# Attention outputs kept transposed: no turns on PE, softmax sums inverted once per batch through DRAM, and the last expert rows of one tile weighted on PE

## What is computed

```python
x = x + 0.5 * ffn(layernorm(x))
x = x + attn(layernorm(x))
x = x + 0.5 * ffn(layernorm(x))

# attn: 32 heads of 16 for q, ONE head of 16 for k and v, ALiBi, causal
q = xn @ Wqkv[:, :512]; k = xn @ Wqkv[:, 512:528]; v = xn @ Wqkv[:, 528:]
scores = q k^T / 4 + slope_h * (pos_k - pos_q), causal
attn = softmax(scores) @ v            # [256, 32 heads * 16]
return attn @ Wo

# ffn: softmax router over 16 experts in 4 groups, 2 groups kept, 2 experts of them
y = sum over the 2 chosen e: gate_e * ((silu(x w1_e + b1) * (x w2_e + b2)) @ w3_e + b3)
return y + shared_expert(x)           # shared: 512 -> 256 -> 512
```

## Time and profile before

| | |
|---|---|
| median of 3 runs | 467.0 us (466.22 to 468.55) |
| the profiled execution, its time | 467.78 us |
| its span in the profile | 466.0 us |
| PE busy | 409.6 us, 88% |
| DVE busy | 261.9 us, 56% |
| ACT / POOL busy | 180.3 / 162.7 us |
| chain that ended last | PE 57%, DVE 15%, DMA 9%, SP's issues 9% |
| mean granted clock of PE | 0.97 of full speed |

### The profile page before, as it was taken

How to read it: one execution, slowest core, us unless ns; L and a number is a source line. 1 busy time by engine, 2 the same in 40 slices (tenths; PEclk the granted TensorE clock), 3 DMA queues, 4 the chain that set the end, 5 groups by cost and what they waited for, 6 DMA issues and landing times.

```text
span 466.0 us, 8466 instructions
## 1 busy us (share of the span) xinstructions
PE 409.6 (88%) x2848; PEld 289.0 (62%) x2849; DVE 261.9 (56%) x729; ACT 180.3 (39%) x300; POOL 162.7 (35%) x230
## 2 busy tenths in 40 slices
PE   0799879999959979879999899798999879999982
PEld 1687567888636757546665465343687558888650
DVE  5489513333258955868885785633239932333347
ACT  1321235665102221146663364483522316665300
POOL 2611316665302852333332242252000054666300
PEclk9999998999979999979999999999999989999987
DMA  7999973534296479212211200020120042444277
GB/s 213 312 372 313 322 234 129 171 108 158 99 364 191 129 181 194 75 39 73 74 56 26 69 6 6 0 74 24 46 91 1 1 134 79 171 132 147 95 269 305
DMA packets 48620, 63.88 MB, mean 137 GB/s; under 512 B 7750, under 2 KB 28070, under 8 KB 48548
## 3 DMA queue, kind: packets, MB, share of 16 engines
q1 hardware_dynamic: 40220, 41.51, 28.2%
q0 software_dynamic: 6368, 19.19, 12.8%
q10 hardware_dynamic: 2000, 2.76, 2.0%
HBM read 46.06 MB, written 19.79 MB: 141 GB/s over the span
## 4 chain that ended last, share of the span: by engine, by line
PE 57%; DVE 15%; DMA 9%; SPq 9%; issue 5%; POOL 2%; ACT 1%; ACTq 0%; POOLq 0%; DVEq 0%
PE ps L1453 14%; PE ps L1460 7%; PE ps L1607 6%; SPq L320 5%; PE ps L1579 5%; PE ps L1438 3%; DMA w<-in_L_ffn_ew_dram 3%; PE ps L1317 3%; PE ps L1522 3%; PE ps L1551 3%; DMA q_dram<-arena 2%; DVE arena L1159 2%; PE ps L1553 2%; PE ps L1565 2%; PE ps L1589 2%
## 5 line engine op out<-in xcount | busy, mean ns | idle before, releaser
L1159 DVE TENSOR_REDUCE arena<-ps 128x3 f32<-128x384 f32 x128 | 67.2, 550 | 17.5 <-PE ps L1553 16.7
L1453 PE MATMUL ps<-arena,wj 128*128 128x128 f32 x608 | 75.5, 278 | 0.0
L1453 PEld LDWEIGHTS ps<-arena,wj 128*128 128x128 f32 x608 | 72.6, 195 | 1.0 <-issue 1.0
L762 ACT ACTIVATE arena<-ps 128x768 f32<-128x768 f32 x64 | 51.8, 811 | 50.7 <-PE ps L1567 49.8
L592 POOL TENSOR_SCALAR_AFFINE_SELECT arena<-arena 128x512 f32<-128x512 f32 x64 | 40.8, 637 | 83.3 <-ACT arena L762 82.9
L1056 DVE SCALAR_TENSOR_TENSOR arena<-ps,arena 128x128 f32<-128x128 f32 x38 | 13.3, 351 | 87.6 <-ACT arena L678 87.6
L1317 PE MATMUL ps<-arena,turns 128*128 128x256 f32 x256 | 57.6, 381 | 0.0
L1317 PEld LDWEIGHTS ps<-arena,turns 128*128 128x128 f32 x256 | 48.2, 190 | 8.1 <-issue 2.1
L524 POOL DMA_INDIRECT y_dram<-arena x38 | 38.4, 1011 | 40.1 <-DVE arena L1063 31.6
L519 POOL DMA_INDIRECT arena<-xn_dram,arena x34 | 33.2, 977 | 51.4 <-DVE arena L996 25.2
L1460 PE MATMUL ps<-w,arena 128*128 x76 | 40.1, 611 | 4.0 <-DVE arena L1056 4.0
(11 more groups left out here) (190 smaller groups left out, 609.7 us busy)
## 6 DMA issues: line engine op xcount, KB each, us to landing
arena<-y_dram SPq DMA_DIRECT2D x16, 512.0 KB, 7.4
arena<-q_dram SPq DMA_DIRECT2D x36, 128.0 KB, 2.6
xn_dram<-arena SPq DMA_DIRECT2D x16, 256.0 KB, 5.8
w<-in_L_ffn_ew_dram SPq DMA_DIRECT2D x4, 1024.0 KB, 10.9
q_dram<-arena SPq DMA_DIRECT2D x16, 192.0 KB, 2.4
x<-_attn_hidden_states_dram SPq DMA_DIRECT2D x4, 512.0 KB, 6.0
...
```

The source lines that it names most:

```text
L762: act.activation(pr[:, n % 2, pair, :], ps[:, bank:bank + 2, :].rearrange("p a b -> p (a b)")[:, 0:768], ACT.Exp).then_inc(sem("exp"), 1)
L1159: dve.tensor_reduce(m3[:, h:h + 1, :], ps[:, bank, 0:3 * P].rearrange("p (n k) -> p n k", n=3), AX_X, ALU.max).then_inc(sem("s_max"), 1)
L1453: ins = pe.matmul(o, wj[:, par, c, n * INTER:(n + 1) * INTER], xgT[:, par, c, :], start=(c == 0), stop=(c == KC - 1))
```

## The change

**Attention without turns.** The output of four heads stays transposed. `vv` now holds v and ones interleaved (1, v0, 1, v1, ...): an even n takes 32 columns from the second on and gets values on the even partitions and the row's sum on the odd ones, an odd n the other way round. ACT copies an even n into `aT[b % 2][:, c, :]` (c = n // 2 % 4) and an odd n into `odd`. SP then moves, SBUF to SBUF: the sums of the even (`sums_of_even`), the sums of the odd and the odd values into their places (`odd_in`, two DMAs). The rows of Wo are loaded in the matching order, in two DMAs. `turn_back`, `attn_turn`, `turned`, `normalise(n)` are gone.

**Sums per batch.** For batches 0 to 2, DVE inverts the packed sums of a batch with one reciprocal of 128x256 (`invert`, in the next batch's q = 2); SP writes them to `r_dram` and reads them back with eight broadcasting DMAs (`inverses`); DVE multiplies the batch's 128x1024 outputs with one instruction (`normalise(b)`, at q = 4). For batch 3 the sums are copied to all rows at once and each pair of groups is inverted and multiplied alone (`normalise_last(c)`).

**Output product.** `out_part(b, t, c)` is a quarter of `out_product`: batches 0 and 1 have theirs in q = 5 (two between s1 and s2), and after the groups 5, 6 and 7; batch 2 after the groups 5 and 6 of the last batch; batch 3 one in the last group and the rest at the end. `max_turn(0, 1)` with its DVE work moves from ahead of the loop into group 0. `residual`, `row_stats`, `ln_stats` and `ln_rows` are spread over other groups.

**FFN.** `y_rows` of tiles 4 to 6 wait for six instead of eight `shared_up`; `shared_h(7)` stands before `pairs_x(1)` in FFN 0. In FFN 1, ACT makes two diagonal matrices of tile 6's gates (`weighing`), and PE adds the tile's expert rows with them to the shared output in PSUM (`rows_in(6)`), so that `pairs_x(6)` is gone and `shared_x(6)` comes after `pairs_x(5)`.

```diff
@@ ffn_sp
-            nc.sync.wait_ge(sem("s_gu"), NT * f + NT)
-            y_rows(range(4, NT))
+            nc.sync.wait_ge(sem("s_gu"), NT * f + NT - 2)
+            y_rows(range(4, NT - 1))
+            nc.sync.wait_ge(sem("s_gu"), NT * f + NT)
+            y_rows((NT - 1,))
@@ att_sp
+            def sums_of_even(p):
+                b, c = p // KC, p % KC
+                last = b + 1 == BATCH
+                sp.wait_ge(sem("oT"), 2 * p + 1)
+                if last and c >= 2:
+                    sp.wait_ge(sem("normed"), b + c - 1)
+                into, rows = (sums[(c + 1) % 2], slice(0, P, 2)) if last else (sums[b % 2], slice(2 * c, P, 32) if c else slice(0, P, 2))
+                sp.dma_start(into[rows], aT[b % 2][rows.start + 1::rows.step, c]).then_inc(sem(f"even_sums{p % 2}"), 16)
+            def odd_in(p):
...
+                sp.wait_ge(sem("oT"), 2 * p + 2)
...
+                sp.dma_start(into[rows.start + 1::rows.step], odd[rows]).then_inc(sem(f"odd_in{p % 2}"), 16)
+                sp.wait_ge(sem(f"even_sums{p % 2}"), 16 * (p // 2 + 1))
+                sp.dma_start(aT[b % 2][1::2, c], odd[1::2]).then_inc(sem(f"odd_in{p % 2}"), 16)
+            def inverses(b):
+                sp.wait_ge(sem("a_rec"), b + 1)
...
+                sp.dma_start(r_dram, sums[b % 2]).then_inc(sem("r_out"), 16)
+                sp.wait_ge(sem("r_out"), 16 * (b + 1))
+                for h in range(4):
+                    for g in range(2):
+                        at = 32 * h + g
+                        sp.dma_start(inverse[at:32 * h + 32:2], r_dram[at:at + 2 * KC:2].partition_broadcast(HD)).then_inc(sem("r_in"), 16)
@@ ffn_act, f == 1, behind the jobs
+                for c in range(CHOICES):
+                    ins = act.activation(weighing[:, c, :], ident, ACT.Copy, scale=etop[:, NT - 2, c:c + 1])
@@ att_act
             def outputs(n):
                 act.wait_ge(sem("pv"), n + 1)
-                if n >= 1:
-                    act.wait_ge(sem("ot"), n)
-                act.copy(oT[:], ps[:, PS_O, 0:SEQ]).then_inc(sem("oT"), 1)
+                if n % 2 == 0:
+                    if b >= 2 and c == 0:
+                        act.wait_ge(sem("a_wo"), QT * (b - 1))
+                    act.copy(aT[b % 2][:, c, :], ps[:, PS_O, 0:SEQ]).then_inc(sem("oT"), 1)
+                else:
+                    if p >= 1:
+                        act.wait_ge(sem(f"odd_in{(p - 1) % 2}"), 32 * ((p - 1) // 2 + 1))
+                    act.copy(odd[:], ps[:, PS_O, 0:SEQ]).then_inc(sem("oT"), 1)
@@ att_dve
+            def invert(b):
...
+                dve.reciprocal(sums[b % 2], sums[b % 2]).then_inc(sem("a_rec"), 1)
+            def normalise(b):
+                dve.wait_ge(sem("r_in"), 16 * 8 * (b + 1))
+                dve.tensor_tensor(aT[b % 2], aT[b % 2], inverse, ALU.mult).then_inc(sem("normed"), 1)
@@ ffn_pe, f == 1
+            def rows_in(t):
+                pe.wait_ge(sem("weighed"), 1)
+                pe.wait_ge(sem(f"yg{t}"), 32)
+                for c in range(CHOICES):
+                    ins = pe.matmul(ps[:, z_bank(t), :], weighing[:, c, :], yg[:, t, c, :], start=False, stop=(c == CHOICES - 1))
@@ att_pe
+            def out_part(b, t, c):
+                pe.wait_ge(sem("normed"), b + 1 if b + 1 < BATCH else b + c + 1)
+                ins = pe.matmul(ps[:, at_bank(b, t), :], aT[b % 2][:, c, t * P:(t + 1) * P], wo[:, c, :], start=(c == 0), stop=(c == KC - 1))
```

More of the change, by code:

```diff
@@ L1252, in att_dve @@
                         maxima_signed(0, 0)
-            maxima_signed(0, 1)
-            maxima_parts(0, 1)
             for b in range(BATCH):
@@ L1265, in att_dve @@
                         maxima(b + 1, 4 * q + 1, PS_S + 1)
-                    if n >= 2:
-                        normalise(n - 2)
+                    if q == 2 and b >= 1:
+                        invert(b - 1)
+                    if q == 4 and not more:
+                        normalise(b - 1)
+                    if q in (4, 6) and not more:
+                        normalise_last(q // 2 - 2)
+                    if q == 6 and b >= 1:
+                        residual(b - 1, 0)
+                    if q == 0 and b >= 2:
+                        residual(b - 2, 1)
                     if more:
@@ L1695, in att_pe @@
+                    if not more:
+                        if q == 5:
+                            pe.wait_ge(sem("s_max"), HEADS * BATCH)
+                        if q in (5, 6):
+                            for c in range(KC):
+                                out_part(b - 1, q - 5, c)
+                        if q == 7:
+                            pe.wait_ge(sem("m_parts"), 2 * b + 2)
+                            out_part(b, 0, 0)
             last = 8 * BATCH - 1
-            turn_back(last - 1)
+            pe.wait_ge(sem("att_x"), QT * (BATCH - 1))
@@ L1697, in att_pe @@
             xn_turn(1, 0)
             weigh(last)
-            xn_turn(1, 1)
-            turn_back(last)
-            xn_turn(1, 2)
-            xn_turn(1, 3)
-            attn_turn(BATCH - 1, 0)
-            pe.wait_ge(sem("oT"), last + 1)
-            attn_turn(BATCH - 1, 1)
+            for t in range(1, 4):
+                xn_turn(1, t)
+            pe.wait_ge(sem("oT"), last + 1)
+            out_part(BATCH - 1, 0, 1)
+            for c in range(KC - 2):
+                out_part(BATCH - 1, 1, c)
@@ L1706, in att_pe @@
+            for t in range(QT):
+                out_part(BATCH - 1, t, KC - 2)
             xn_turn(1, 4)
-            out_product(BATCH - 1, 0)
             xn_turn(1, 5)
-            out_product(BATCH - 1, 1)
+            for t in range(QT):
+                out_part(BATCH - 1, t, KC - 1)
             pe.wait_ge(sem("exp"), 2 * 8 * BATCH)
```

206 lines of the change are left out of this document (107 added, 99 removed).

## The result

| | before | after |
|---|---|---|
| median of 4 runs each, taken side by side | 466.6 us | 473.1 us |
| ratio, 95% interval | | 1.014 (1.010 to 1.018) |
| the profiled execution, its time | 467.78 us | 475.97 us |
| its span | 466.0 us | 474.2 us |

The forecast was 458.0 us, with 466 as the upper end of its range. The change costs about 6.5 us where 9 were expected to be saved. From here on Wn is the weighing issued in group n (W1 the first, W24 that of the last batch's first group), and "before" and "after" are the two kernels.

A forecast was written before the change was run, and what follows sets the result against it. PE, nearly always busy in the attention loop, and its waits were taken as the bound. Terms -2.4 - 2.9 + 1.6 - 3.9 - 1.4 = -9.0 us, off the 467.0 median, gave 458.0 us (8 in 10: 451.5 to 466).

The forecast's parts named there:

- the clock: Half-speed PE after stalls of about 3 us: 1.3 us added per stall, with 0 and 2 as ends.
- the chain: Sums' copy, write, eight reads at 0.35 us, multiplication: 2.2 us lost in each of two batches; PE stands 3.6 in batch 3.
- C's base: C without the chain and its clock: groups -6.7 us, reciprocals +1.3 us.
- A: End of FFN 0: `shared_h(7)` ahead of `pairs_x(1)` starts later work earlier, -2.4 us (-1 to -3.2).
- B: Start of the attention loop: `max_turn(0,1)` behind group 0 removes PE's 2.12 us wait and half clock, -2.9 us (-1.5 to -3.5).
- D's base: D, batch 3 and its end, without the chain's wait and its clock: 31.0 us forecast.
- E: End of FFN 1: two DVE additions of 0.75 us go, PE's products cost part of it, -1.4 us (-2.5 to +0.3).
- C: Groups 2 to 24 of the attention loop: turns saved against reciprocal, chain and clock, +1.6 us (-5 to +9).
- D: Batch 3 to its last output product: shorter groups and end, less a chain wait and clock, -3.9 us (-7.5 to +1).
- Rival 3: The chains are longer: SP pays 0.64 us an issue and the clock is lost each time, 462 to 469 us; chance 0.24.
- The reciprocal: DVE's 128x256 reciprocal in q = 2: 1.4 us, making the group's end 0.65 late, twice, +1.3 us.
- Rival 4: SP becomes the bound: ACT's odd copies wait for the pair before to leave `odd`, 474 to 478 us; chance 0.06.

The follow-up runs named there:

- h2_halves: The kernel of experiment 6 with the 128x256 reciprocal of batches 0 and 1 split into two halves of 128x128: 452.6 us, ratio to before 0.970.
- experiment 3: The changed kernel with its three 128x256 reciprocals replaced by products of the same size: 473.9 us, ratio to before 1.016.
- experiment 6: Changed kernel with four reads, multiplication a group later, old FFN 1 end; SP's next-pair copies moved from behind the reads to between write and reads: 454.1 us.
- e4_no_reciprocal: The kernel of experiment 3: the changed kernel with products in place of the three reciprocals, 473.9 us.
- g2_before_A: The kernel before with only `shared_h(7)` moved ahead of `pairs_x(1)` in FFN 0: ratio to before 0.994.
- h1_odd_between: The kernel of experiment 6, with SP's next-pair copies between the write and the reads: 454.1 us, ratio to before 0.975.

## Why the prediction was wrong

The miss, 473.1 less 458.0, is 15.1 us. The kernel without the round trip divides it: the prediction's terms make that kernel 446.1 us (458.0 less two waits of 2.2, one of 3.6 and three times 1.3 for the clock, 11.9 together), and it took 454.7 (451.9 to 456.9 in four runs). So 8.6 us were missed in the rest of the kernel, and 6.5 us in the chain, which cost 18.4 where 11.9 were forecast. The chain is the largest single error, but not the greater half; the rest is C's base (4.4), A and B (2.1), D's base (2.0) and E (0.5), as worked out below, which is 9.0 by the profiles and means.

**A held in size, not in its way.** In after PE started the projections 3.7 us earlier, at 139.56 against 143.26 us, and stood 2.52 us ahead of `xa_turn` without losing its clock; before had stood longer, 4.75 us. But that profile lost most of it again: at 185 us PE waited 2.08 us for the maxima and came back at half clock (0.67 in the mean of 184 to 190 us), so that the loop began 0.9 us earlier only (200.53 against 201.46). The other profiles of kernels with A have W2 at 205.1 to 207.6 us, after 208.8. The forecast followed the gain only to the next step.

**B was overestimated.** Its first half, the earlier start of the loop, was partly a change of place of DVE's work, as shown above; its second, the clock, was lost in one profile of the old order and kept in another. A and B together were put at 5.3 us; the runs give 3.2 (1.9 to 4.5).

**C's base, +4.4 us.** Without the round trip W2 to W24 takes 86.0 us where the sum of groups and reciprocals had 81.6. Two steps are as large as 1 us. The groups W12 to W13 and W20 to W21 took 6.35 us each where the terms give 5.47 (3.76 and two quarters, 1.71): PE waits 1.6 us there for the multiplication alone, 1.2 us of DVE. The prediction had seen a part of it (PE at 7.5, DVE's reads only at about 8.3 without the chain), took these 0.8 us off the chain's price and never put them into the groups: 1.6 us in the two batches, a slip of the sum. The group behind the reciprocal of batch 1 took 4.7 instead of 3.5. Plain groups stayed at 2.88 us; I had derived 2.83 from DVE's read, and the turn had been hidden altogether (about 1 us in all). The rest is tenths in many groups, up and down.

**The chain of the sums: the step that failed.** By stages it cost 3.6 us more than forecast in C (1.4 of them the group W10 to W11 above) and 4.4 us more in D. The way was forecast as it happened, and each PE wait stood where the text looks for it; the term that was mis-sized is the length of the chain, above all SP's price of a read, 0.35 us where it took 0.64. With t = 0 at the weighing of q = 2, 233.90 us in batch 1 and 275.01 in batch 2:

| | forecast | batch 1 | batch 2 |
|---|---|---|---|
| write issued | 2.4 | 4.0 | 2.5 |
| write landed | 4.4 | 6.0 | 4.5 |
| eight reads issued | 7.2 (0.35 each) | 11.1 (0.64 each) | 10.0 |
| product over | 10.5 | 14.1 | 13.0 |
| PE is there | 7.5 | 11.2 | 8.6 |
| PE waited | 3.0 (2.2 of it the chain's) | 3.0 | 4.6 |

The price of the reads is there in both batches. The late write is not: in batch 1 SP was in `m_rows` till 235.5 us and only then copied the sums of the even output (L434), which the last copy of `odd_in` waits for; in batch 2 that copy had gone at 273.41, ahead of t = 0. And in batch 1 the wait of 3.0 us is the forecast one by luck: the chain was 3.6 us late, and PE itself 3.7, behind the reciprocal.

Rival 3 named 0.64 us an issue, and gave 462 to 469: it had the right row, and the same terms for the rest of the kernel. The prediction has no reason for its 0.35 except that `m_rows` with its small pieces had 0.27. In after the reads of `m_rows` (3x16x128) still take 0.29 each and nearly everything else on SP 0.5 to 0.64: the upper row was the one to take. In batch 3 the groups are so short that all of the lateness is PE's: 7.1 instead of 3.6 us, and the eight products behind it run at half clock.

**The clock** was put at 1.3 us for each of three waits. It was lost four times: 1.9 us in batch 1 (3.75 for 1.88), 1.6 in batch 2 (3.48), about 3 in batch 3 (6.65 for 3.70), 6.4 together where 3.9 were put, and some more behind the reciprocal.

**The reciprocal** took 1.75 us, I had 1.4. The Trainium skill, page "VectorE: DVE Perf Modes", section "Walkthrough: the 8-slice pipeline in each mode", has the repeat count of 8 from which the estimate of 2.2 us came. The trace lies between that and my 1.4: 1.75 us for 256 elements a partition and 0.94 for 128 (`h2_halves`), 6.3 ns an element. It was not worth an argument: without it the time was the same (experiment 3).

**D's base, +2.0 us**, is what 33.0 us without the round trip leave over the forecast's 31.0; the same stage scatters by 2.6 us over four profiles of the old attention, so its cause stays open. **E** was put at -1.4 us and is -0.9 by the means (21.8 against 22.7), and after's own profile was longer (23.3): the gain comes from the earlier loads, which I gave nothing, and not from PE's products, to which I gave all. That its size is near is luck.

**The rivals.** Rival 3 is the nearest, above its range. Rival 4 did not occur in after but does exist: it appeared as soon as the chain stood ahead of the copies on SP, and the order of experiment 6 took PE's wait for it away. The chances had put 0.09 on slower. Errors of one sign that share a cause, SP's price of an issue, enter three chains at once and bring the clock with them; I had treated the ends of the terms as if they were independent.

## What to carry over

A DMA chain that replaces work on a busy engine costs its latency, and a good part of that is the issuing engine: count issues, at the price of a long row of them, and put first what the chain's start waits for. If the result is wanted a few groups later, and other issues fit in the time in which the write lands, the same chain is nearly free: 473.1 us became 452.6 with the write and the reads still there, four for eight, where after without them, the multiplication at its old place, had 454.7. At the end of FFN 1 the move of work to an idle engine, with the last step hanging on two more engines, gained nothing on average. And a forecast of many small gains should be checked without its largest cost: here that part alone was 8.6 us too low.

## What the runs showed of the chip

- An issue on SP took 0.47 to 0.64 us for 4x256, 64x256, 16x4x256 and 32x1024 elements alike, and 0.29 for 3x16x128; twice the bytes a DMA at half the count halved the time (5.1 to 2.5 us).
- A reciprocal of 128x256 float32 took 1.75 us and one of 128x128 0.94, where the three products of 128x256 in its place (`e4_no_reciprocal`) took 0.43, 0.52 and 0.87.
- The same wait of about 2.1 us was followed by the lower of the two clocks in one profile (0.50 from 203 to 207 us in before) and not in another (1.00 in `g2_before_A`), with the same instructions around it. Waits of 3.0, 4.6 and 7.1 us in after were each followed by half clock, a wait of 2.5 us at 134 us was not. At one place, behind the first reciprocal, PE kept its clock in four profiles with waits of 1.42, 1.63, 1.76 and 1.79 us (the group took 4.4 to 4.7 us) and lost it in four with 1.83, 1.87, 2.05 and 2.21 (5.2 to 6.1 us). The waits of 2.12 and 2.5 us after which it was kept show that the length alone doesn't decide; these runs don't show what does.
- Profiles of kernels with `shared_h(7)` early had W2 anywhere from 205.1 to 208.8 us; in after PE waited 2.08 us at 185 us, in `h1_odd_between` 2.30 us, and both lost their clock behind it (0.50 from 187 to 189 us); in the others it waited up to 1.4 us there and kept it.

```profile
185.35 0.28 PE L1635 MATMUL ps<-cb 128*128 128x256 bf16 x1 [2.08 <-DVE arena L1208]
184.97 0.28 PE L1632 MATMUL ps<-cb 128*128 128x256 bf16 x1 [2.30 <-DVE arena L1206]
```
